# Order of gathers and scatters in GpSimd's queue, row buffers and pair weights in the sparse experts of a two-layer decoder

## What is computed

```python
logits = einsum('bsh,eh->bse', x, router_w) + expert_bias
scores = softmax(logits)
top_w, top_idx = top_k(scores, 4)
top_w = top_w / sum(top_w)
g = einsum('bsh,khe->bske', x, gate_proj)
u = einsum('bsh,khe->bske', x, up_proj)
out = einsum('bske,keh->bskh', silu(g) * u, down_proj)
sel = take_along_axis(out, top_idx[..., None], axis=2)
return sum(sel * top_w[..., None], axis=2)
```

## Time and profile before

| | us |
|---|---|
| three runs | 4879.73, 4889.91, 4893.45 (median 4889.91) |
| profiled execution | 4875.86 |
| its span | 4874.1 |
| front part of `routed_experts`, first load to first gather | 847.1 to 920.1 |
| first gather to last scatter issued | 920.1 to 1578.8 |
| reading back and joining | 1582.4 to 1602.2 |

### The profile page before, as it was taken

One profiled execution on the slowest core, in us unless ns is written; L12 is line 12 of the kernel. 1 busy time (PEld: TensorE's weight loads), 2 busy tenths in 40 slices (PEclk: granted clock), 3 DMA queues, 4 the chain that ended last, 5 costly groups with the idle time before them and its releaser, 6 DMA issues. The chain is left out here.

```text
span 4874.1 us, 58249 instructions
## 1 busy us (share of the span) xinstructions
PE 3685.5 (76%) x17574; PEld 2826.0 (58%) x17574; DVE 2718.5 (56%) x7933; ACT 1613.8 (33%) x4118; POOL 1557.5 (32%) x2243
## 2 busy tenths in 40 slices
PE   6999964555655579999999999994799999970230
PEld 4667743433333468888888888883466566550130
DVE  4666643410000378888888888864566666655023
ACT  2444321011111244555555455441344444430010
POOL 0000000133333154555555555560111111115547
PEclk9999986677676699999999999997899999985565
DMA  1000012212122201111111111111000000003150
GB/s 64 0 0 0 0 51 54 67 32 34 31 33 33 58 19 39 39 23 37 31 35 36 23 37 36 29 19 56 1 0 0 0 0 0 0 12 107 49 149 14
DMA packets 225351, 152.21 MB, mean 31 GB/s; under 512 B 125496, under 2 KB 211702, under 8 KB 224096
## 3 DMA queue, kind: packets, MB, share of 16 engines
q1 hardware_dynamic: 192880, 113.99, 9.1%
q0 software_dynamic: 27456, 30.91, 3.5%
q10 hardware_dynamic: 4800, 4.72, 0.3%
HBM read 117.41 MB, written 56.11 MB: 36 GB/s over the span
## 5 line engine op out<-in xcount | busy, mean ns | idle before, releaser
L1867 DVE SCALAR_TENSOR_TENSOR dl_y<-ps,dl_taps,dl_y 128x255 f32<-128x255 f32 (+2 forms) x1536 | 652.6, 474 | 129.5 <-ACT dl_y L1763 125.3
L1598 PE MATMUL ps<-xnT,dl_wkqv 128*128 128x256 f32 x2048 | 543.0, 391 | 26.5 <-DVE dl_lp L1910 23.2
L1598 PEld LDWEIGHTS ps<-xnT,dl_wkqv 128*128 128x128 f32 x2048 | 368.4, 193 | 77.2 <-issue 37.1
L366 POOL TENSOR_TENSOR at_rs<-at_ss,mhalf 128x15 f32<-128x15 f32 x32 | 125.5, 3921 | 746.0 <-DVE at_ss L553 746.0
L1213 DVE COPY moe_xT<-ps 128x256 f32<-128x256 f32 x79 | 33.6, 425 | 586.3 <-PE ps L1044 586.3
L1521 POOL TENSOR_TENSOR dl_rn<-dl_n,mhalf 128x4 f32<-128x4 f32 x128 | 173.3, 1354 | 546.0 <-DVE dl_n L1883 546.0
L452 PE MATMUL ps<-at_shared,at_v 128*128 128x256 f32 (+2 forms) x1280 | 316.3, 380 | 4.6
L1763 ACT ACTIVATE dl_y<-ps,dl_taps 128x256 f32<-128x256 f32 x512 | 260.2, 560 | 101.4 <-PE ps L1598 101.4
L428 PE MATMUL ps<-at_kT,at_qT 128*128 128x320 f32 (+2 forms) x1024 | 271.3, 397 | 2.8 <-ACT at_kT L658 2.8
L1539 POOL TENSOR_TENSOR dl_inv_u<-dl_inv_u,dl_inv_tmp 64x30 f32<-64x30 f32 (+14 forms) x480 | 259.3, 540 | 37.6
L452 PEld LDWEIGHTS ps<-at_shared,at_v 128*128 128x128 f32 (+1 forms) x1280 | 211.4, 191 | 89.6 <-issue 64.2
(11 more groups left out here) (332 smaller groups left out, 8279.8 us busy)
## 6 DMA issues: line engine op xcount, KB each, us to landing
dl_grow<-decay_rows SPq DMA_DIRECT2D x128, 128.0 KB, 3.1
sp_wgu<-in_w1gu SPq DMA_DIRECT2D x12, 768.0 KB, 11.0
dl_wkqv<-in_w1kqv SPq DMA_DIRECT2D x16, 512.0 KB, 5.0
delta_diag<-dl_lp SPq DMA_DIRECT2D x512, 8.0 KB, 1.5
dl_diag<-delta_diag_tt SPq DMA_DIRECT2D x512, 8.0 KB, 1.7
moe_wgu<-in_w0gu SPq DMA_DIRECT2D x16, 448.0 KB, 11.7
slot_rows<-sp_zero SPq DMA_DIRECT2D x4, 1152.0 KB, 8.1
sp_wd<-in_w1d SPq DMA_DIRECT2D x12, 384.0 KB, 11.3
```

The source lines that it names most:

```text
L1598: last = nc.tensor.matmul(bank(h, m // 2, (m % 2) * S, (m % 2 + 1) * S), wkqv[h][:, c, m * P:(m + 1) * P], k.xnT[:, c, u.seq * S:(u.seq + ...
L1867: last = nc.vector.scalar_tensor_tensor(y[h][:, m, back:S], bank(h, m // 2, (m % 2) * S, (m % 2 + 1) * S - back), taps[h][:, m, KC - 1 - b ...
```

## The change

Three edits in `routed_experts`:

1. RX goes from 4 to 8 row buffers `xs`.
2. GpSimd's queue: six gathers are issued first, and then `fetch(i+6)` stands ahead of `add(i)` in every step, where before `fetch(i+3)` stood ahead of `add(i)`.
3. The seven VectorE instructions that spread the weights over the experts, with the signal `weighed`, move from behind the one-hot loop to right behind the normalised weights. The last of the seven is now waited for before the signal goes out.

```diff
-    RX, RH, RY = 4, 2, 4
+    RX, RH, RY, AHEAD = 8, 2, 4, 6
...
-                for i in range(TILES + 3):
-                    if i < TILES:
-                        fetch(i)
-                    if i >= 3:
-                        add(i - 3)
+                for i in range(AHEAD):
+                    fetch(i)
+                for i in range(TILES):
+                    if i + AHEAD < TILES:
+                        fetch(i + AHEAD)
+                    add(i)
...
+                for j in range(TOPK0):
+                    last = nc.vector.tensor_tensor(part[:, :, j, :], eq[:, :, j, :],
+                                                   ex[:, :, j:j + 1].to_broadcast([P, NT, E0]), ALU.mult)
+                ch.link(last)
+                nc.vector.tensor_tensor(part[:, :, 0, :], part[:, :, 0, :], part[:, :, 1, :], ALU.add)
+                ch.link(nc.vector.tensor_tensor(part[:, :, 2, :], part[:, :, 2, :], part[:, :, 3, :], ALU.add))
+                ch.link(nc.vector.tensor_tensor(rows[:, :, D:W], part[:, :, 0, :], part[:, :, 2, :], ALU.add))
+                dve.sem_inc(weighed, 1)
+
                 dve.wait_ge(counted, 1)
...
-                for j in range(TOPK0):
-                    last = nc.vector.tensor_tensor(part[:, :, j, :], eq[:, :, j, :],
-                                                   ex[:, :, j:j + 1].to_broadcast([P, NT, E0]), ALU.mult)
-                ch.link(last)
-                nc.vector.tensor_tensor(part[:, :, 0, :], part[:, :, 0, :], part[:, :, 1, :], ALU.add)
-                ch.link(nc.vector.tensor_tensor(part[:, :, 2, :], part[:, :, 2, :], part[:, :, 3, :], ALU.add))
-                nc.vector.tensor_tensor(rows[:, :, D:W], part[:, :, 0, :], part[:, :, 2, :], ALU.add).then_inc(weighed, 1)
```

## The result

| | runs | median us | ratio to before, 95% interval |
|---|---|---|---|
| before | 4 | 4891.68 (4879.73 to 4895.68) | |
| changed | 4 | 4500.35 (4489.30 to 4505.73) | 0.9201 (0.9175 to 0.9227) |

391.3 us less, 8.0%; 4495 was predicted, with 4456 to 4580 as the range. The profiled execution of the changed kernel took 4505.4 with a span of 4503.6.

What follows compares the result with a forecast made beforehand. A closed ring over GpSimd's queue, 8.37 us a tile, bound the kernel. At 3.25 a tile the terms gain 394.9: 4875.86 becomes 4481.0, and the median, 14.05 above the profiled run, 4495; range 4456 to 4580.

Steps and rivals of the forecast that it cites:

- The ring and its end: Tile loop: scatter waits for y, product, turn, gather and previous scatter, 8.37 us a tile; six gathers ahead would open this.
- GpSimd as the bound: Tile loop after the change: GpSimd's scatter 1.89 plus gather 1.36, 3.25 us a tile, the largest of the engines.
- The reserve of 5.5: Gather n to scatter n: GpSimd's own work 20.9 us against the data's 15.4, so y waits for GpSimd.
- first gather earlier, against the store of x: Start of the loop: with early weights the first gather waits for the index alone, at 918.2, gaining 1.9 us.
- first gather to first scatter: Start of the loop, while TensorE warms up: 18.24 us as before, so first scatter at 936.5.
- first scatter to last gather: Tile loop: one scatter of 1.89, then 71 times gather and scatter, 230.75; predicted 232.6 us in all.
- last gather to last scatter: End of the loop: gather 1.36, then seven scatters spaced by landings, 13.4; predicted 14.8 us in all.
- contention with VectorE: Tile loop: GpSimd's DMA instructions beside VectorE might take longer, 0 to +41 us; taken as 0.
- The rival of exclusion: Tile loop: each GpSimd DMA instruction waits out VectorE's work, 0.97 a tile, period 4.22, time 4571; 8%.
- the low clock: Tile loop: short gaps keep TensorE at its lower level, 5.62 a tile, 4680; whole 6%, mixed up to +60, 12%.
- the closed ring: Tile loop: the ring closes again over a wait called passed, period 4.8, time 4616; 3%.
- the late landing: Shared DMA queue: scatters land late behind gathers and hold up later gathers; at a landing of 20, 5043; 1%.

Runs made afterwards that it cites:

- e2: Changed kernel with four gathers ahead of a scatter in place of six: 4536.50 us, ratio 0.9305.
- e1: Changed kernel with five gathers ahead of a scatter in place of six: 4491.85 us, ratio 0.9206.
- e3: Changed kernel with four row buffers in place of eight, still six gathers ahead: 4491.13 us, ratio 0.9203.
- e4: Changed kernel with the weight-spreading block back behind the one-hot loop: 4488.40 us, ratio 0.9206.
- e5: Kernel before with only the weight-spreading block moved early, old queue order and four buffers: 4895.48 us, ratio 1.0002.
- e6: Changed kernel without the scatters of the odd tiles and the waits for their landing: 4465.23 us, ratio 0.9134.
- e7: Changed kernel with one of the two halves of the `down` product left out: 4501.89 us, ratio 0.9207.
- e11: The changed kernel run once more, without any further edit: 4497.24 us, ratio 0.9206.
- e9: Changed kernel with scatters that overwrite in place of adding: 4507.61 us, ratio 0.9221.

## Why the prediction was right

**The ring and its end.** The step that carried the sum was that the kernel waits in a closed ring over GpSimd's queue, and that with six gathers ahead it is longer than needed. e2 and e1 show it from both sides, e3, e4 and e5 that it is the order alone.

**GpSimd as the bound.** Forecast 3.25 a tile, measured 3.26 (228.27/70). Gather n to scatter n was worked out as 20.9; in the tiles that I followed it is 20.93 to 20.94. From gather to the end of y I had 14.6; it is 14.5 to 15.0 in all of these but one. The reserve of 5.5 and the 0.81 from y to a scatter make 6.3, and 5.9 to 6.5 is what the trace shows. e6 and e7 show the bound by taking work from either engine.

**The terms of the sum**, each in the profiled execution. They come from one trace each, and the interval of the ratio is 25 us wide, so the runs by themselves can't tell any of the differences in this table:

| term | predicted | measured |
|---|---|---|
| first gather earlier, against the store of x | 1.9 | 1.5 (69.9 to 68.4) |
| first gather to first scatter | 18.2 | 20.0 |
| first scatter to last gather | 232.6 | 233.5 |
| last gather to last scatter | 14.8 | 14.8 |
| last scatter to the end of the join (1209.07 + 4.91) | 23.4 | 23.8 |
| gain in the function | 394.9 | 391.5 |

The term that was most mis-sized is the second. I took over the 18.2 of the kernel before as if it belonged to the work; the 1.8 it is longer are one more `up` product at the lower clock (3.35 against 1.67), and over the traces this stretch goes from 15.5 to 20.0 with the clock. That the sum of the other terms came within 2 us is the forecast's merit; where in these 4.5 us the second term fell is chance (with e11's 15.9 the gain in the function is 394.0). The first term is 0.4 short since the index came 0.3 later than forecast and the first gather 0.9 behind it, not 0.8. The median came out 5.35 above the 4495: 1.77 because the median before is 4891.68 over four runs and not 4889.91, the rest in the gain.

**Costs that the trace didn't show.** Taking zero for the contention with VectorE was right: GpSimd's DMA instructions ran with VectorE busy for 61.24 of 228.27 us and kept their 1586 and 1059 ns. The rival of exclusion stood at 4571, and no run here shows it. The rule of the Trainium skill cited ahead (SBUF — State Buffer, "SBUF: two separate sides") doesn't ask for all of the 0.97 a tile either: it speaks of VectorE's instructions in a 2-port mode or, beside a GpSimd instruction that reads SBUF, of those with two inputs in SBUF. Here only `take_weight` has two inputs in SBUF; `keep_x` and `gate` read PSUM, and nothing here shows them in such a mode. An estimate for that one alone, from the earlier trace rows, is 0.168 x 78 = 13 us, and the unchanged 1586 and 1059 ns show none of it. It is a statement on this mix alone.

**The rivals.** The exclusion fell by those two means, the low clock by the granted 0.99 and by e7, the closed ring by the 20.93 us, and the late landing by the group of the scatters: 2.0 us of waiting for one another in the whole loop. What was not foreseen is that TensorE stood 0.45 below GpSimd, not 0.34: its tile takes 2.81 once every product is warm (e6), the 2.91 of the earlier trace rows began behind an idle stretch of 0.60, with an `up` of 1.77 in place of 1.67. TensorE's wait for a gather, forecast at about 0.3 a tile, is 14.4/79 = 0.18.

## What to carry to other kernels

Where every engine is half idle, look for the ring in one in-order queue, count how many tiles it spans, and compare its length divided by that number with the busiest engine's own cost a tile: that gives the lead needed (here five) and the new bound before anything is built. With the new order more buffers bought nothing (e3), and a lead of six in place of five nothing that the runs can tell (e1); what it buys is reserve, which hides stalls. More buffers with the old order were not run; its gathers never waited for one (their idle time in the earlier trace rows is all issue), so nothing is to be expected of them. Take from a trace the time of the stage that was edited, since the rest of the program can differ by more than the edit's smaller parts.

## What the runs showed of the hardware

- An indirect scatter of 128 rows of 1 KB takes GpSimd 1.59 us if it adds (the changed kernel) and 1.03 if it overwrites (e9), about what a gather takes (1.04 to 1.06). The next DMA instruction starts 0.30 later, if nothing is waited for; when the queue stood still waiting, it starts 0.8 to 0.9 after the end of the instruction that it waited for (0.81 behind y, 0.92 behind the index).
- The time to landing must be read for the right transfer. For the changed kernel the profile has no time to landing for the gathers and scatters at all. The view of the table `expert_rows` gives a median of 6.8 us there, and the expectation of e1 took this for the gathers; it is the middle of SyncE's two stores into that table, the zeros (line 967) and the rows (line 969):

```profile
DMA to landing us min/median/max: 5.1/5.1/5.1
```

```profile
DMA to landing us min/median/max: 8.5/8.5/8.5
```

  In e1, whose trace has a time for the gathers (line 987), it is 2.9:

```profile
DMA to landing us min/median/max: 2.8/2.9/4.9
```

  That fits the changed kernel, in which TensorE began to turn rows as soon as 2.9 us after their gather had started.
- TensorE at its bound was now and then held up for some 3 us (e9), and not at all with half of the scatters left out (e6). The cause stays open.
